# Two sixteen-head attentions in a program of four blocks: preparation shared out anew, and copies of ScalarE and VectorE in another order

## What is computed

```python
q, k, v = x @ Wq, x @ Wk, x @ Wv                  # 16 heads of 8 channels
r = sin_rpe(2 * L - 1) @ Wr                       # one row per distance
ac = einsum('bqhd,bkhd->bhqk', q + u_bias, k)
bd = rel_shift(einsum('bqhd,rhd->bhqr', q + v_bias, r))
out = softmax((ac + bd) / sqrt(8)) @ v
```

## Time and profile before

| what | value |
|---|---|
| median of 3 runs | 6683.83 us (6681.53 to 6688.11) |
| profiled execution | 6683.83 us |
| its span, first to last instruction | 6682.0 us |
| PE busy over the span | 5185.6 us (78%) |
| DVE busy | 4402.4 us (66%) |
| ACT busy | 3186.9 us (48%) |
| POOL busy | 2034.1 us (30%) |
| mean granted TensorE clock | 0.872 |

### The profile page before, as it was taken

How to read it: one execution, slowest core, us unless ns; L and a number is a source line. 1 busy time by engine, 2 the same in 40 slices (tenths; PEclk the granted TensorE clock), 3 DMA queues, 4 the chain that set the end, 5 groups by cost and what they waited for, 6 DMA issues and landing times. The chain is left out here.

```text
span 6682.0 us, 113234 instructions
## 1 busy us (share of the span) xinstructions
PE 5185.6 (78%) x33132; PEld 3585.6 (54%) x33132; DVE 4402.4 (66%) x10941; ACT 3186.9 (48%) x5879; POOL 2034.1 (30%) x1374
## 2 busy tenths in 40 slices
PE   6776888877769979867769979974859648496777
PEld 5664455466657737625546746743534436342663
DVE  6996677689967747736657747746836259363774
ACT  6775777667755535535555535533020330303223
POOL 6995111089944324212114414400020000300110
PEclk8998999989989989989999989995569755698888
DMA  1000888600000000000000000000010000200000
GB/s 28 0 0 3 258 274 269 206 15 0 0 11 0 0 14 0 3 6 1 1 11 1 0 14 1 0 3 14 7 45 0 1 14 0 51 0 14 0 0 16
DMA packets 162591, 213.91 MB, mean 32 GB/s; under 512 B 54804, under 2 KB 90984, under 8 KB 162408
## 3 DMA queue, kind: packets, MB, share of 16 engines
q1 hardware_dynamic: 160360, 207.73, 10.2%
q0 software_dynamic: 2048, 4.20, 0.2%
HBM read 104.91 MB, written 106.95 MB: 32 GB/s over the span
## 5 line engine op out<-in xcount | busy, mean ns | idle before, releaser
L1807 POOL TENSOR_TENSOR l0b_S<-l0b_sim 128x1024 f32<-128x1024 f32 x256 | 494.3, 1970 | 148.9 <-ACT l0b_sim L1870 124.7
L1807 POOL TENSOR_TENSOR l0a_S<-l0a_sim 128x1024 f32<-128x1024 f32 x256 | 494.3, 1969 | 83.7 <-ACT l0a_sim L1870 62.7
L1842 PE MATMUL l0b_WT<-ident,l0b_w 128*128 128x128 f32 x2048 | 269.1, 288 | 65.7 <-DVE l0b_w L1940 61.0
L1842 PE MATMUL l0a_WT<-ident,l0a_w 128*128 128x128 f32 x2048 | 267.9, 286 | 64.2 <-DVE l0a_w L1940 59.3
L1940 DVE SCALAR_TENSOR_TENSOR l0a_w<-l0a_S,l0a_best,l0a_SG 128x1024 f32<-128x1024 f32 x256 | 311.2, 1276 | 8.2 <-ACT l0a_SG L1887 4.4
L1940 DVE SCALAR_TENSOR_TENSOR l0b_w<-l0b_S,l0b_best,l0b_SG 128x1024 f32<-128x1024 f32 x256 | 311.2, 1276 | 8.3 <-ACT l0b_SG L1887 4.4
L1842 PEld LDWEIGHTS l0b_WT<-ident,l0b_w 128*128 128x128 f32 x2048 | 240.6, 148 | 108.9 <-DVE l0b_w L1940 108.9
L1842 PEld LDWEIGHTS l0a_WT<-ident,l0a_w 128*128 128x128 f32 x2048 | 238.7, 147 | 108.1 <-DVE l0a_w L1940 108.1
L1887 ACT ACTIVATE l0b_SG<-l0b_S 128x1024 f32<-128x1024 f32 x256 | 260.1, 1024 | 57.1 <-DVE l0b_w L1940 52.1
L1887 ACT ACTIVATE l0a_SG<-l0a_S 128x1024 f32<-128x1024 f32 x256 | 260.0, 1024 | 54.8 <-DVE l0a_w L1940 49.3
L769 ACT ACTIVATE l0att_XS<-l0att_XP 128x768 f32<-128x768 f32 x256 | 223.9, 874 | 115.1 <-PE l0att_XP L623 109.1
(11 more groups left out here) (707 smaller groups left out, 14409.9 us busy)
## 6 DMA issues: line engine op xcount, KB each, us to landing
shifted_rows<-l0att_XS SPq DMA_DIRECT2D x256, 384.0 KB, 3.8
l0att_BD<-shifted_rows SPq DMA_DIRECT2D x256, 256.0 KB, 3.5
enter_raw<-L_attn_w SPq DMA_DIRECT2D x4, 512.0 KB, 6.9
token_rows<-l2ar_rows SPq DMA_DIRECT2D x32, 64.0 KB, 1.5
l2ae_wgt<-L_ffn_gate_w SPq DMA_DIRECT2D x32, 64.0 KB
l2ae_wut<-L_ffn_up_w SPq DMA_DIRECT2D x32, 64.0 KB
l2ae_wdt<-L_ffn_down_w SPq DMA_DIRECT2D x32, 64.0 KB
token_rows<-l2br_rows SPq DMA_DIRECT2D x32, 64.0 KB, 1.5
```

The source lines that it names most:

```text
L1807: pool.tensor_tensor(S[:, h, :].rearrange("p (a c) -> p a c", a=NK), a, c, ALU.add).then_inc(sm["summed"], 1)
L1842: o = pe.matmul(WT[:, n // 4, (n % 4) * P:(n % 4 + 1) * P], w[:, h % W_RING, n * P:(n + 1) * P], ident[:, :], start=h == 0 and n % 4 == 0, ...
```

## The change

The first part moves work of the preparation. DVE clears `spread`; POOL stages the first `xs` as its first instruction and clears only the two last columns of each strip. PE waits only for the loads and `xs`, makes the distances' projection and then at once the first sequence's projection; the split of the distances is done by DVE in a tile of its own (`rwhole`), and DVE prepares (rel) or rotates (rope) the first sequence ahead of its steps. The steps begin at -6, since the projections that steps -9 to -7 held are now ahead.

The second part is order. In the rope kind ACT does both heads' exponentials and then the copy of the strips. In the rel kind PE spreads "v" ahead of the second head's transposes and the scores, and DVE copies the strip ahead of the second head's turned block, and the first head's turned block ahead of `keep_out`. The number of products, copies and DMAs per pair is unchanged.

```diff
--- before.py
+++ after.py
@@ -446,6 +446,7 @@
         if rel:
             ub, vb = ph.sb("ub", [P, 1]), ph.sb("vb", [P, 1])
             wr, emb = ph.sb("wr", [P, P]), ph.sb("emb", [P, 2 * L])
+            rwhole = ph.sb("rwhole", [P, 3, 2 * L])
             rpart = ph.sb("rpart", [P, 3, 2 * L], BF)
             RP = ph.sb("RP", [P, G, 2 * L], BF)
             XS = ph.sb("XS", [P, 2, 2, WIN, 2])
@@ -476,7 +477,7 @@
             return not isinstance(b, int) or 0 <= n < NB
 
         def steps(eng, step):
-            for j in range(-10, BEGIN):
+            for j in range(-6, BEGIN):
                 step(0, j)
             with eng.Fori(0, NB // 2 - 1) as b:
                 for j in range(BEGIN, BEGIN + 16):
@@ -534,8 +535,8 @@
 
             @block.gpsimd
             def _(pool):
-                pool.memset(spread[:, :, :, :, :, :, :].rearrange("p w k g r c d -> p (w k g r c d)"), 0.0).then_inc(sm["prepared"], 1)
-                pool.memset(strips[:, :, :, :], 0.0).then_inc(sm["cleared"], 1)
+                pool.tensor_copy(xs[:, :], XN[:, 0:L]).then_inc(sm["staged"], 1)
+                pool.memset(strips[:, :, :, L:L + 2], 0.0).then_inc(sm["cleared"], 1)
                 pool.memset(V[:, :, :, :, :], 0.0).then_inc(sm["cleared"], 1)
                 pool.wait_ge(sm["cleared"], 2)
                 pool.memset(V[:, :, :, :, HD:HD + 1], 1.0).then_inc(sm["cleared"], 1)
@@ -577,13 +578,6 @@
                     in_parts(sm["split"], whole[:, :, :], (rest1[:, :, :], rest2[:, :, :]),
                              [part[:, par, k, :, :] for k in range(3)], 5 * n)
 
-                if rel:
-                    pool.wait_ge(sm["rp_kept"], 1)
-                    pool.sem_inc(sm["passed"], 1)
-                    two = (lambda x: x[:, 0:2, :].rearrange("p w n -> p (w n)"))
-                    in_parts(sm["rp_split"], two(whole), (two(rest1), two(rest2)), [rpart[:, k, :] for k in range(3)], 0)
-                    pool.wait_ge(sm["rp_split"], 5)
-                stage(0)
                 split(0, 0)
                 stage(1)
                 split(1, 1)
@@ -594,11 +588,7 @@
 
             @block.tensor
             def _(pe):
-                pe.wait_ge(sm["loaded"], loads)
-                pe.wait_ge(sm["prepared"], 2)
-                pe.wait_ge(sm["cleared"], 3)
-                if rel:
-                    pe.matmul(EX[:, :], wr[:, :], emb[:, :], start=True, stop=True).then_inc(sm["rp_made"], 1)
+                def distances():
                     pe.wait_ge(sm["rp_split"], 5)
                     for g in range(G):
                         if g >= 2:
@@ -737,9 +727,9 @@
                     distance_rows(b, j + 3, 1)
                     if j % 2 == 1:
                         values(b, j - 2)
+                    spread_out(b, j + 5, "v")
                     turn(b, j - 1, 1)
                     scores(b, j + 1)
-                    spread_out(b, j + 5, "v")
                     extras(b, j)
 
                 def rope_step(b, j):
@@ -751,6 +741,19 @@
                     spread_out(b, j + 5, "qk")
                     extras(b, j)
 
+                pe.wait_ge(sm["loaded"], loads)
+                pe.wait_ge(sm["staged"], 1)
+                if rel:
+                    pe.matmul(EX[:, :], wr[:, :], emb[:, :], start=True, stop=True).then_inc(sm["rp_made"], 1)
+                    pe.wait_ge(sm["rp_kept"], 1)
+                project(0, wq, wk).then_inc(sm["projected"], 1)
+                if not rel:
+                    pe.wait_ge(sm["parts_made"], 1)
+                    project(0, wqx, wkx).then_inc(sm["crossed"], 1)
+                pe.wait_ge(sm["prepared"], 2)
+                pe.wait_ge(sm["cleared"], 3)
+                if rel:
+                    distances()
                 steps(pe, rel_step if rel else rope_step)
 
             @block.scalar
@@ -794,7 +797,10 @@
                     g, n = j % G, 2 * b + j // G
                     keep_rows(b, j + 3, 0)
                     raise_up(b, j, 0)
-                    keep_strips(b, j + 5)
+                    if rel:
+                        keep_strips(b, j + 5)
+                    else:
+                        raise_up(b, j, 1)
                     keep_rows(b, j + 3, 1)
                     if not rel and g in (2, 6):
                         keep_out(b, n - (g == 2), int(g == 2))
@@ -806,17 +812,33 @@
                         until(act, sm["valued"], 4 * n + 2)
                         act.activation(V[:, (j // G + 1) % 2, :, :, 0:HD],
                                        EX[:, 0:L].rearrange("p (c h d) -> p c h d", c=2, h=NH), ACT.Copy).then_inc(sm["v_copied"], 1)
-                    raise_up(b, j, 1)
+                    if rel:
+                        raise_up(b, j, 1)
+                    else:
+                        keep_strips(b, j + 5)
 
                 steps(act, step)
 
             @block.vector
             def _(dve):
                 dve.sem_inc(sm["added"], 1)
+                dve.memset(spread[:, :, :, :, :, :, :].rearrange("p w k g r c d -> p (w k g r c d)"), 0.0).then_inc(sm["prepared"], 1)
                 dve.wait_ge(sm["loaded"], loads)
-                if rel:
+
+                def distances():
+
                     dve.wait_ge(sm["rp_made"], 1)
-                    dve.tensor_copy(whole[:, 0:2, :], EX[:, :].rearrange("p (w n) -> p w n", w=2)).then_inc(sm["rp_kept"], 1)
+                    dve.tensor_copy(rwhole[:, 0, :], EX[:, :]).then_inc(sm["rp_kept"], 1)
+                    dve.wait_ge(sm["rp_kept"], 1)
+                    for n in range(3):
+                        if n > 0:
+                            dve.wait_ge(sm["rp_split"], 2 * n)
+                        dve.tensor_copy(rpart[:, n, :], rwhole[:, n, :]).then_inc(sm["rp_split"], 1)
+                        if n < 2:
+                            dve.wait_ge(sm["rp_split"], 2 * n + 1)
+                            dve.tensor_tensor(rwhole[:, n + 1, :], rwhole[:, n, :], rpart[:, n, :], ALU.subtract).then_inc(sm["rp_split"], 1)
+
+                def keep_distances():
                     for g in range(0, G, 2):
                         dve.wait_ge(sm["rp_spread"], g + 1)
                         if g > 0:
@@ -889,9 +911,9 @@
                     shift(b, j, 0)
                     if not rel:
                         shift(b, j, 1)
+                    keep_turned(b, j - 1, 0)
                     if g in (2, 6) and rel:
                         keep_out(b, n - (g == 2), int(g == 2))
-                    keep_turned(b, j - 1, 0)
                     if g == 0 and inside(b, n + 1):
                         if rel:
                             prepare(n + 1)
@@ -905,9 +927,16 @@
                         residual(n - 1)
                     if rel:
                         shift(b, j, 1)
+                    keep_strips(b, j + 5)
                     keep_turned(b, j - 1, 1)
-                    keep_strips(b, j + 5)
-
+
+                if rel:
+                    distances()
+                    prepare(0)
+                    keep_distances()
+                else:
+                    rotate(0, 0)
+                    rotate(0, 1)
                 steps(dve, step)
```

## The result

The changed kernel takes **6536.76 us** (median of 4 runs, 6533.97 to 6552.68) against 6685.97 us of the kernel before on the same chip: a ratio of 0.9781, 95% interval [0.9762, 0.9799]. The profiled run took 6533.99 us with a span of 6532.2 us.

The account below looks back on a forecast made before the run. The prediction took PE plus its waits to bound both phases; savings of 20 + 9 + 58 + 20 = 107 us from 6683.8 gave 6577 us, with a range of 6538 to 6628.

Parts of the forecast that it names:

- What bounds each phase: Both phases' steps: PE plus its waits; in rope a circle through ACT's strips' copy, one turn 2.95 us.
- Preparation, rel: Start of rel: first spread product moves from 661.12 to 640.6, saving 20 us (bounds 16 and 22).
- Preparation, rope: Start of rope: first projection moves from 2963.71 to about 2955.0, saving 9 us (7 to 9.5).
- about 21 us: Sign in rope's preparation: first 6-fold spread product about 21 us rather than 27 us behind the phase's start.
- Order, rope: Rope steps: with strips' copy behind all four exponentials, PE's 58.6 us of waits lose their cause; 58 us saved (30 to 80).
- 10 us of new waits for shifts: Rope steps: PE gets 10 us of new waits for shifts, offsetting 10 us let go from waits for ACT's copies.
- Order, rel: Rel steps: strips' copy wait of 11.9 us vanishes and v product fills a gap; 20 us saved (0 to 35).
- DMA or the new wait for the strips holds rel: Rival, rel steps: rel gains nothing, from high transfer share or v product waiting for ACT; 6597 us, chance 0.13.
- the floor by the share: Rel steps: at a DMA share of 0.84 the transfers need 526 us of the 626.6.
- DVE takes over in rope: Rival, rope steps: PE waits 0.4 us for shifts in 64 steps without `values`, about 28 us back; 6605 us, chance 0.15.
- PE runs full in rope: Rival, rope steps: waits for ACT shrink too; rope gains 80 us and rel 35; 6540 us, chance 0.10.
- The slower rival: Rel steps: a circle through v product, scores, shift, exponentials and strips closes, lengthening all 128 steps; 6712 us at 0.9 us each, chance 0.03.

Follow-up runs that it names:

- The version with the strips' copy third: Changed kernel with SyncE's row reads five DMAs behind their writes, and in rope strips' copy after both heads' exponentials, before OT, oT, V copies: 6529.35 us, 0.9762.
- reads later: Changed kernel with SyncE reading each row block five DMAs behind its write instead of three: 6492.53 us, 0.9699 of the kernel before.
- the half of the pair that was run: Changed kernel with reads later and PE's v product in rel back behind the scores, DVE keeping its new order: 6537.89 us, 0.9786.
- the slowest version: Changed kernel with reads later and, in rel too, ACT's strips' copy behind both heads' exponentials: 6794.72 us, 1.0172 of the kernel before.

## Why the prediction was right or wrong

- **What bounds each phase** was right for rope: the circle through the strips' copy, and with it the sign and the place of the gain. For rel it was wrong: I read PE and its waits, and left SyncE's queue out of the argument. The kernel before already shows SyncE waiting 238.4 us for its writes to land and DVE 24.1 us for rows. The first figure alone would have proved nothing: with the same code in these steps it was 188.5 us in the kernel with ACT's order alone and 147.3 in the one with the preparation alone, and the steps were no shorter.
- **Preparation, rel** (20, bounds 16 to 22; measured 25.7). Up to the first spread product it is 22.3 us, just above its bounds: 19.65 us behind the phase's start instead of 41.94 (forecast 21.4). The split took 2.8 us for 3.8, and the distance products 7.02 for 8.32. The last 3.4 us I had not counted: the six spread products take 0.83 us where they took 1.46, and PE is at the higher clock, granted 1.00 from there to the first scores against 0.54 before. Ahead of them PE has run the distance products; in the kernel before it stood idle 7.71 us. The memset of `spread` took 2.62 us for an estimated 2.9. The rule of the Trainium skill ("SBUF — State Buffer", "Who interferes with whom", on the shared port pair) showed no effect. The page names copies, casts and operations with a scalar operand as able to take the pair, and operations with two SBUF inputs against reads of GpSimd, but no memset for this chip, so for the memset the prediction had stretched it. The rest did not meet: POOL's copy of `xs` ran before DVE's memset had started, POOL's memsets of V took 1.79 and 0.21 us beside it (1.81 and 0.21 before), and POOL's casts, 3.85 us for 3.88, ended 1.2 us before DVE began to split. That the two would wait for one another if they met with reads on both sides, no run here shows.
- **Preparation, rope** (9; measured 8.6): right, step by step. The first spread product came 18.2 us behind the phase's start, as 27 - 9 gives; the "about 21 us" among the signs did not fit the term.
- **Order, rope** (58, bounds 30 to 80; measured 110). The mechanism was right, and the size was wrong in two places. The first is "The other waits, 48.6 us, are for copies of ACT (OT, V, oT) ... I let 10 us of them go". They fell to 12.3 us, 26 more than forecast. With the strips' copy ahead of OT, V and oT all three waits are back in full and the phase takes 41.5 us more, so what makes them come sooner, instead of 0.74 us later, is that the strips' copy stands behind them. The second is that only waits were counted: PE's own busy time fell too, from 365.27 to 332.46 us for the same products, 33 us, at a granted clock of 0.99 for 0.96, and the sum had it at nothing. The "10 us of new waits for shifts" came about (2.8 to 13.3 us), and 6.9 us of waits for POOL's parts are new: 52 us more than forecast is 26 + 33 less those 7. The prediction's own step times came nearer: 2.95 to 2.3 us in 64 bare steps and 3.7 to 2.8 in 64 with `values` are 99 us, which it argued down to 58. Even its 2.3 us was long; a bare step can take 1.91, since DVE's mean of 2.48 us a pair holds the work of other steps too. The version with the strips' copy third gained 72 us, which is within the bounds of 30 to 80.
- **Order, rel** (20, bounds 0 to 35; measured a loss of 1.6, and 1.0001 by itself). This is the rival "DMA or the new wait for the strips holds rel", and both halves of it are seen: PE's 94.7 us for the strips, DVE's 86.5 us for rows. But its reason, "the transfers' share is high already", falls: with reads later the same transfers run at a share of 0.88 and 289 GB/s, and the steps take 52 us less. The limit was the time from a write to the read behind it in one serial queue. On the floor by the share (526 us) or by the bandwidth that the Trainium skill, "Perfetto Trace Analysis", on identifying the most-contended engine, recommends instead (464 us, an estimate from the skill): 572.5 us lies above both, so no run here decides between them. Neither was the bound in the change: at a share of 0.85 the steps could still lose 52 us, which agrees with the page's doubt about occupancy.
- **The rivals.** "DVE takes over in rope" took nothing (13.3 us of waits for shifts; its own price, 0.4 us in 64 steps, is 26 us and not 28). "PE runs full in rope" had the right rope, with a gain of more than 80 us, for the reason that it gave, but not its 35 us in rel. The slower rival, a circle through the v product and the strips in rel, does not close in the change (4.88 us a step); it closes when ACT's copy is moved back there as well, at 6.8 us a step.

Against the forecast, rel's preparation gave 6 us more, rel's order 22 us less, rope's order 52 us more and the other phases 7 us more. The misses cancel in part, and that the total comes so near the range is partly luck: of the two orders one missed its bounds above and one below.

## What to carry to other kernels

Before reordering engines, follow each wait to its far end, serial DMA queues too: an order that frees PE is worth nothing (here within 4 us) while a read waits in its queue for a write issued three DMAs earlier, and 42 us once it waits for one issued five earlier. When a circle through an in-order engine is found, list what else stands in that engine's queue: the same move that opened the circle also brought three other copies forward, for another 41.5 us, and done in the neighbouring phase, where a product stands behind the moved copy, it costs 300 us. Orders of two engines that hand work to each other are tried together, for the half of the pair that was run gained nothing by itself.

## What the runs showed of the hardware

- **Where PE waited more, its products took longer too.** The same rope products kept PE busy 332.5 us at a mean granted clock of 0.99, 365.3 at 0.96 and 408.0 at 0.91; the same rel products 490.2 us at 0.99 and 588.6 at 0.85. The first pair grew by 10% for 3% of the clock, so the mean clock is not the whole of it; what the rest is, no run here separates.

```profile
2950.40:3556.10 605.70, 407.98 (x3363) 260.74 (x3364) 317.04 (x1371) 271.27 (x693) 87.09 (x105) 0.91 0.00 1
655.00:1528.20 873.20, 588.63 (x4886) 367.40 (x4886) 462.04 (x1543) 483.01 (x895) 92.12 (x89) 0.85 0.58 190
```

- **The two levels of the clock, 2.4 and 1.2 GHz, stand side by side in the preparations of the changed kernel.** In rel (first line) six spread products take 0.83 us; PE had been busy 6.87 of the 8 us before. In rope (second line) the same six take 1.44 us behind 7.01 us of idle time, and 1.46 behind only 0.69 at 2939.01, so it is the level of the stretch that counts and not the idle time just before.

```profile
636.00:648.40 12.40, 8.75 (x75) 4.85 (x77) 1.70 (x4) 7.41 (x11) 0.40 (x1) 1.00 0.40 119
2936.00:2946.00 10.00, 7.05 (x33) 4.04 (x33) 0.00 (x0) 2.73 (x5) 0.81 (x2) 0.50 0.00 0
2936.88 1.44 PE L649 MATMUL l1att_PJ<-l1att_part,l1att_spread 128*128 128x256 bf16 x6 [7.01 <-POOL l1att_part L563]
```

- **How long a DMA takes to land did not follow the transfers' share.** The median from issue to landing of the same 384 KB write was 4.2 us in the change (share 0.85) and 3.2 us with reads later (share 0.88, the line below), and 2.5 us in the slowest version (share 0.58). The order of the queue is not all that sets it: three kernels with the rel steps of before had 3.8, 3.3 and 3.0 us (before, ACT's order alone, preparation alone).

```profile
shifted_rows<-l0att_XS SPq DMA_DIRECT2D x256, 384.0 KB, 3.2
```
